# Turning the second block's row maxima on VectorE instead of TensorE

## The chip, the cores and the metric

One core of a Trainium2 chip runs the kernel. Its engines work side by side, each through its own list of instructions in order: TensorE (PE), VectorE (DVE), ScalarE (ACT), GpSimd (POOL) and the queue of SyncE (SP), which issues all transfers. They meet in counting semaphores. The metric is the device time of one execution in microseconds (us), as the median of several runs.

## The reference, cut to what matters

```python
scale = cond @ norm_w.T + 1.0
ms = mean(x * x, axis=-1)
h = x * (scale[:, None, :] * rsqrt(ms + EPS))
u = h @ up_w.T                                  # up_w: 4096 x 512
val, gate = split(u, 2, axis=-1)
h = val * gelu(gate)                            # 4096 rows x 2048
s = 127 / max(max|h| over the row, 1e-5)
hq = clip(round(h * s), -128, 127) / s          # one scale for each row
wq = clip(round(down_w * t), -1, 1) / t         # t: one scale for all of down_w
y = hq @ wq.T + x
```

x has 4 x 1024 rows of 512 numbers. The part around the change is `s`: the row's largest |h|, and from it the row's scale.

## The kernel before, in words

The 4096 rows are worked on in 8 blocks of 512 (`b` = 0 to 7; "second block" is `b` = 1). In a block the hidden dimension 2048 goes in J = 16 tiles of 128. So there are 128 tiles, numbered `n = 16 b + j`. A tile lies with the hidden dimension on the partitions and the block's 512 rows along the free dimension (128x512). Every engine runs one loop over `n`, and its order is written out by hand.

**Tiles 32 to 127** (blocks 2 to 7) make the up product with seven half-size products instead of eight, each in three fp16 passes (lines 582 to 584, 128x256 matmuls of which one starts every 0.11 us). Between the products stand sums that other engines make: ScalarE copies two halves (L803, L806), VectorE adds `seed_gate(n)` (L1135, into `ps_g`) and `second_val(n)` (L1140, into `ps_v`). In round `n` TensorE runs first_pair(n), third(n-1) (waits for seed_gate(n-1)), gates(n-1), second(n), fourth(n-1) (waits for second_val(n-1)). Each round has 42 of these matmuls, 4.58 us. In the first rounds of a block TensorE also makes a quarter of the down product of the block before last (16 matmuls of L709, 3.45 us).

**VectorE** in round `n`: `hidden(n-2)` (L1152: val times gelu), `second_val(n-1)`, `scaled` (L1230: h of the block before times the row scales that stand in the PSUM tile `ps_m`), `peak_of(n-2)` (L1162, L1165: running maximum `h_max`), `residual` (L1251), `seed_gate(n)`, `rounded` (L1237), `sum_low` (L1061), `row_dequant` in round 5 of a block (L1219 or L1223), the norm of the next block (L1101) and the differences of its operands (L1110 to L1124, L1130). `sum_low(k)` belongs to the weights' sums, which are made once, in tiles 20 to 40: POOL sums four parts (L970 to L976), ScalarE makes the high part (L874), VectorE the low part (L1061); SyncE loads the next part (L408) when a buffer is free after `sum_low`. In the third block (tiles 32 to 47) sums 11 to 15 fall in tiles 34, 35, 37, 38 and 40, and all differences of the next block stand in tile 34:

```python
if j == 2:
    difference(b + 1, XT1)
if j == (2 if b < 3 else 4):
    difference(b + 1, XT2)
```

**From the row maxima to the scales.** After the last tile of block `b`, h_max[128, 512] holds for every row 128 partial maxima, one on each partition. There are two ways to the scales, chosen by `by_vector(b)`, which is `V_FIRST <= b < NB - 1`.

- By TensorE (blocks 0, 1 and 7 before): in tile 1 of the next block `turn_max` turns h_max by four transposes into ps_m (L692); in tile 2 VectorE's `row_scales` reduces it (L1206) and makes the scale in three small steps (L1209 to L1213), ahead of its `hidden`; TensorE's `spread_scale` spreads the scales over the partitions by four more transposes (L698).
- By VectorE (blocks 2 to 6 before): in tile 1 `turn_peaks` transposes h_max in 32x32 squares (L1172) and reduces it (L1174); in tile 2, behind `seed_gate`, `spread_peaks` gathers the four quarters with three copies (L1182), reduces them and makes the scale (L1185 to L1193), spreads it with three copies (L1196) and writes ps_m by one transpose (L1200). `row_dequant` then takes four instructions (L1223) instead of one (L1219).

Of the kernel before, what the change touches and what calls it, by code (L numbers as in the profile page):

```python
# [43 lines left out]
def bass_cond_norm_geglu_bitlinear(  # L44
# [83 lines left out]
    RS_DRAM = 5  # L128


    V_FIRST = 2

    def h_home(b, j):
        return J + j if j < 2 and b % 2 == 1 else j
# [1 line left out]
    with ExitStack() as ctx:  # L136
# [176 lines left out]
        def by_vector(b):  # L313
            return V_FIRST <= b < NB - 1

# [710 lines left out]
        def _(dve):  # L1026
# [77 lines left out]
            def difference(c, k):  # L1104
                before = (c - 2) * 4
                if k == XT1:
                    dve.wait_ge(xn_ready, c * KT + 2)
                    if by_vector(c - 2):
                        dve.wait_ge(peak_step, (c - 2 - V_FIRST) * PEAK_STEPS + 1)
                    dve.tensor_tensor(ta[:], xt[:, 0:2, HB:TB], xt[:, 0:2, 0:HB], ALU.subtract).then_inc(t_ready, 1)  # L1110
# [66 lines left out]
            def spread_peaks(b):  # L1177

                base = (b - V_FIRST) * PEAK_STEPS
                dve.wait_ge(peak_step, base + 1)  # L1180
# [249 lines left out]
```

## Time and profile before

| | |
|---|---|
| median of 3 runs | 746.95 us (746.33 to 747.03) |
| the profiled execution | 748.39 us, of which its span is 746.6 us |
| TensorE busy | 732.8 us (98%) |
| VectorE busy | 561.1 us (75%) |
| ScalarE busy | 347.8 us (47%) |
| GpSimd busy | 97.9 us (13%), all before 238 us |

The span runs from the first to the last instruction that the profiler recorded; 1.79 us of the execution lie around it. Times in the rows below are counted from the span's start. The timeline view gives for each entry its start, its length and, in brackets, how long the engine had been idle before it and what ended that.

### The profile page before, as it was taken

What the parts mean: (1) busy time and instruction counts of PE and PEld (TensorE: products, weight loads), DVE (VectorE), ACT (ScalarE), POOL (GpSimd) and SP (SyncE); (2) the same over time, 40 slices, a digit from 0 to 9 for tenths busy, and PEclk for the clock granted to TensorE, in tenths of its full rate; (3) what the DMA queues carried; (4) which work ended last, traced back from release to release, by engine and by line L of the source; (5) the groups of instructions that cost most, each with busy time, mean ns of one, the idle gap of its engine ahead of it and who ended that gap; (6) DMA issues with size and microseconds to landing.
All of it is one profiled execution on the core that took longest, in us unless ns stands there. A gap on an engine that the chain in (4) does not pass through costs nothing.

```text
span 746.6 us, 14329 instructions
## 1 busy us (share of the span) xinstructions
PE 732.8 (98%) x5480; PEld 536.6 (72%) x5480; DVE 561.1 (75%) x1126; ACT 347.8 (47%) x677; POOL 97.9 (13%) x137
## 2 busy tenths in 40 slices
PE   6999999999999999999999999999999999999998
PEld 5544444444677887888778887788878887688864
DVE  5577778998599776888668775887758876586657
ACT  4888866443164532454324643355424442144424
POOL 1211377763314000000000000000000000000000
PEclk9999999999999999999999999999999999999999
DMA  8887574656546444343533444353443333353202
GB/s 321 292 280 235 176 274 135 234 165 233 205 136 183 156 155 149 117 144 99 196 122 126 129 135 157 116 166 104 149 156 103 100 100 125 123 177 103 97 29 84
DMA packets 44788, 117.33 MB, mean 157 GB/s; under 512 B 5424, under 2 KB 5680, under 8 KB 43568
## 3 DMA queue, kind: packets, MB, share of 16 engines
q1 hardware_dynamic: 44720, 116.42, 47.2%
q8 instruction: 43, 0.70, 0.4%
q14 instruction: 25, 0.20, 0.1%
HBM read 99.62 MB, written 16.78 MB: 156 GB/s over the span
## 4 chain that ended last, share of the span: by engine, by line
PE 88%; DVE 5%; ACT 2%; issue 2%; DMA 1%; SPq 0%; DVEq 0%; POOL 0%; ACTq 0%
PE ps_v L582 14%; PE ps_v L584 14%; PE ps_v L583 14%; PE ps_y L709 12%; PE ps_g L582 6%; PE ps_g L584 6%; PE ps_g L583 5%; PE ps_v L600 3%; PE ps_v L602 3%; PE ps_g L602 3%; PE ps_v L601 3%; PE ps_g L601 3%; PE ps_g L600 3%; PE ps_v L778 1%; DMA q<-in_up_t_dram 1%
## 5 line engine op out<-in xcount | busy, mean ns | idle before, releaser
L582 PE MATMUL ps_v<-x_hi,w_hi 128*128 128x256 f16 x968 | 263.9, 273 | 2.9 <-DVE ps_v L1140 1.9
L584 PE MATMUL ps_v<-x_hi,w_lo 128*128 128x256 f16 x968 | 263.8, 273 | 0.0
L583 PE MATMUL ps_v<-x_lo,w_hi 128*128 128x256 f16 x968 | 263.8, 273 | 0.0
L803 ACT COPY ps_g<-ps_v 128x256 f32<-128x256 f32 x96 | 34.3, 357 | 214.9 <-PE ps_v L584 214.9
L814 ACT ACTIVATE g<-ps_g,w_unscale 128x512 f32<-128x512 f32 x128 | 87.3, 682 | 69.5 <-PE ps_g L584 69.4
L1140 DVE TENSOR_TENSOR ps_v<-ps_v,p 128x256 f32<-128x256 f32 x96 | 41.3, 431 | 97.7 <-PE ps_v L584 97.4
L821 ACT ACTIVATE g<-h 128x512 f32<-128x512 f32 x128 | 81.3, 635 | 57.9 <-DVE h L1152 57.4
L582 PEld LDWEIGHTS ps_v<-x_hi,w_hi 128*128 128x128 f16 x968 | 94.7, 98 | 17.9 <-DVE ps_v L1140 2.9
L584 PE MATMUL ps_g<-x_hi,w_lo 128*128 128x256 f16 x392 | 106.8, 273 | 0.0
L582 PE MATMUL ps_g<-x_hi,w_hi 128*128 128x256 f16 x392 | 106.8, 273 | 0.0
L583 PE MATMUL ps_g<-x_lo,w_hi 128*128 128x256 f16 x392 | 106.8, 273 | 0.0
L583 PEld LDWEIGHTS ps_v<-x_lo,w_hi 128*128 128x128 f16 x968 | 94.7, 98 | 13.4
L584 PEld LDWEIGHTS ps_v<-x_hi,w_lo 128*128 128x128 f16 x968 | 94.7, 98 | 11.0
L709 PE MATMUL ps_y<-dw,q 128*128 128x512 bf16 x448 | 101.3, 379 | 0.0
L1152 DVE SCALAR_TENSOR_TENSOR h<-ps_v,w_unscale,g 128x512 f32<-128x512 f32 x128 | 95.3, 744 | 2.4 <-PE ps_v L584 2.2
L1165 DVE TENSOR_TENSOR h_max<-g,h_max 128x512 f32<-128x512 f32 x120 | 84.6, 705 | 12.9 <-ACT g L821 10.2
L1230 DVE TENSOR_TENSOR h<-h,ps_m 128x512 f32<-128x512 f32 x128 | 83.7, 677 | 1.8 <-PE ps_m L698 1.8
L709 PEld LDWEIGHTS ps_y<-dw,q 128*128 128x128 bf16 x448 | 43.8, 98 | 46.8
L1135 DVE TENSOR_TENSOR ps_g<-ps_v,p 128x256 f32<-128x256 f32 x96 | 41.2, 429 | 22.0 <-PE ps_v L584 20.8
L1237 DVE TENSOR_SCALAR q<-h 128x512 bf16<-128x512 f32 x112 | 52.6, 490 | 0.0
L600 PE MATMUL ps_g<-x_hi,w_hi 128*128 128x512 f16 x124 | 47.0, 379 | 0.0
L601 PE MATMUL ps_g<-x_lo,w_hi 128*128 128x512 f16 x124 | 47.0, 379 | 0.0
(139 smaller groups left out, 925.0 us busy)
## 6 DMA issues: line engine op xcount, KB each, us to landing
w_lo<-w_lo_dram SPq DMA_DIRECT2D x96, 448.0 KB, 3.3
q<-in_up_t_dram SPq DMA_DIRECT2D x16, 512.0 KB, 4.9
xt<-in_x_cols_dram SPq DMA_DIRECT2D x8, 1024.0 KB, 4.9
res<-in_x_rows_dram SPq DMA_DIRECT2D x26, 256.0 KB, 3.4
out_dram<-res SPq DMA_DIRECT2D x26, 256.0 KB, 2.7
sums<-in_up_t_dram SPq DMA_DIRECT2D x12, 512.0 KB, 4.7
xs<-in_x_rows_dram SPq DMA_DIRECT2D x22, 256.0 KB, 3.7
w_lo_dram<-w_lo SPq DMA_DIRECT2D x16, 256.0 KB, 4.4
```

What stands on the lines that cost most here:

```text
L582: pe.matmul(to, w_hi[:, wh:wh + P], hi, start=start and kt == 0, stop=False, skip_group_check=True)
L583: pe.matmul(to, w_hi[:, wh:wh + P], lo, start=False, stop=False, skip_group_check=True)
L584: last = pe.matmul(to, w_lo[:, wl:wl + P], hi, start=False, stop=(kt == 1), skip_group_check=True)
L600: pe.matmul(bank, w_hi[:, wh:wh + P], hi, start=start and kt == 0, stop=False)
L601: pe.matmul(bank, w_hi[:, wh:wh + P], lo, start=False, stop=False)
L709: last = pe.matmul(ps_y[:, i % 2, :], q[:, j * TB + i * P:j * TB + (i + 1) * P], dw[:, j * D:(j + 1) * D], start=(j == 0), stop=(j == J - 1))
L814: act.activation(g[:, n % 3, :], ps_g[:, n % NG, :], ACT.Gelu, scale=w_unscale[:, n % J:n % J + 1]).then_inc(g_ready, 1)
L821: act.activation(g[:, n % 3, :], h[:, at:at + TB], ACT.Abs).then_inc(h_abs_ready, 1)
L1152: dve.scalar_tensor_tensor(out=h[:, at:at + TB], in0=ps_v[:, n % NV, :], scalar=w_unscale[:, j:j + 1], in1=g[:, n % 3, :], op0=ALU.mult, o ...
L1165: dve.tensor_tensor(h_max[:], g[:, n % 3, :], h_max[:], ALU.max).then_inc(h_max_ready, 1)
L1230: dve.tensor_tensor(h[:, at:at + TB], h[:, at:at + TB], ps_m[:], ALU.mult).then_inc(scaled_ready, 1)
L1237: dve.tensor_scalar(to[:, j * TB:(j + 1) * TB], h[:, at:at + TB], ROUND, ROUND, ALU.add, ALU.subtract).then_inc(q_ready, 1)
```

## The change

Block 1 too goes by VectorE. On TensorE the calls turn_max(1) and spread_scale(1) go; on VectorE row_scales(1) goes, and turn_peaks(1), spread_peaks(1) and the four-piece form of row_dequant(1) come.

```diff
@@ -128,7 +128,7 @@
     RS_DRAM = 5
 
 
-    V_FIRST = 2
+    V_FIRST = 1
 
     def h_home(b, j):
         return J + j if j < 2 and b % 2 == 1 else j
```

## Rows read from the trace of the kernel before

**Rows 1.** Waits of TensorE over the whole span: us, times, longest.
```profile
PE ps_v L582 <- DVE ps_v L1140: 1.9, 2, 1.5
...
PE ps_v L582 <- DVE ps_g L1135: 0.2, 1, 0.2
```

**Rows 2.** Busy time by stretch: stretch, its length, then each engine.
```profile
230.00:235.00 5.00, 4.90 (x44) 3.93 (x43) 5.00 (x9) 2.89 (x5) 2.00 (x3) 1.00 0.60 166
235.00:240.00 5.00, 3.48 (x33) 2.89 (x31) 5.00 (x9) 1.21 (x2) 2.43 (x3) 1.00 0.28 93
...
292.00:736.00 444.00, 444.00 (x3702) 362.18 (x3701) 332.15 (x703) 181.37 (x382) 0.00 (x0) 1.00 0.38 123
```

**Rows 3.** Timeline of TensorE around the eight transposes of block 1.
```profile
203.82 0.60 PE L692 MATMUL ps_m<-ident,h_max 128*128 128x128 f32 x4
204.25 0.27 PE L582 MATMUL ps_v<-x_hi,w_hi 128*128 128x256 f16 x1
...
212.29 0.60 PE L698 MATMUL ps_m<-ident,row_peak 128*128 128x128 f32 x4
```

**Rows 4.** Timeline of VectorE, tiles 34 and 35.
```profile
204.45 0.69 DVE L1206 TENSOR_REDUCE row_peak<-ps_m 128x4 f32<-128x512 f32 x1 [1.49 <-PE ps_m L692]
...
205.70 0.75 DVE L1152 SCALAR_TENSOR_TENSOR h<-ps_v,w_unscale,g 128x512 f32<-128x512 f32 x1
...
208.38 0.43 DVE L1135 TENSOR_TENSOR ps_g<-ps_v,p 128x256 f32<-128x256 f32 x1
209.49 1.28 DVE L1061 SCALAR_TENSOR_TENSOR xs<-sums,w_scale,w_hi 128x1024 f16<-128x1024 f32 x1 [0.67 <-ACT w_hi L874]
210.69 0.69 DVE L1110 TENSOR_TENSOR ta<-xt 128x512 f32<-128x512 f32 x1
...
218.49 0.42 DVE L1135 TENSOR_TENSOR ps_g<-ps_v,p 128x256 f32<-128x256 f32 x1
```

**Rows 5.** Timeline of TensorE: its waits for VectorE in tiles 35 to 39.
```profile
218.97 0.28 PE L582 MATMUL ps_v<-x_hi,w_hi 128*128 128x256 f16 x1 [0.18 <-DVE ps_g L1135]
...
222.17 0.28 PE L582 MATMUL ps_v<-x_hi,w_hi 128*128 128x256 f16 x1 [0.41 <-DVE ps_v L1140]
...
238.06 0.28 PE L582 MATMUL ps_v<-x_hi,w_hi 128*128 128x256 f16 x1 [1.52 <-DVE ps_v L1140]
```

**Rows 6.** Timeline of VectorE, the turn and the spreading of block 2.
```profile
294.44 0.70 DVE L1172 STREAM_TRANSPOSE ta<-h_max 128x512 f32<-128x512 f32 x1
...
295.78 0.74 DVE L1152 SCALAR_TENSOR_TENSOR h<-ps_v,w_unscale,g 128x512 f32<-128x512 f32 x1
...
299.50 0.43 DVE L1135 TENSOR_TENSOR ps_g<-ps_v,p 128x256 f32<-128x256 f32 x1 [0.33 <-PE ps_v L584]
299.97 0.55 DVE L1182 COPY tb<-tb 32x16 f32<-32x16 f32 x3
...
302.87 0.69 DVE L1110 TENSOR_TENSOR ta<-xt 128x512 f32<-128x512 f32 x1
```

**Rows 7.** Timeline of VectorE, both forms of row_dequant and what follows.
```profile
229.88 0.68 DVE L1219 TENSOR_SCALAR dequant<-row_peak,d_mean 128x4 f32<-128x4 f32 x1
230.48 0.74 DVE L1152 SCALAR_TENSOR_TENSOR h<-ps_v,w_unscale,g 128x512 f32<-128x512 f32 x1
...
317.39 0.97 DVE L1223 TENSOR_SCALAR dequant<-row_peak,d_mean 32x4 f32<-32x4 f32 x4
318.39 0.75 DVE L1152 SCALAR_TENSOR_TENSOR h<-ps_v,w_unscale,g 128x512 f32<-128x512 f32 x1
```

**Rows 8.** Timelines of the SP queue and of POOL: the weights' sums.
```profile
210.80 0.33 SPq L408 DMA_DIRECT2D sums<-in_up_t_dram  x1
...
215.82 0.73 POOL L970 TENSOR_TENSOR sums<-sums 128x256 f32<-128x256 f32 x1 [13.45 <-DMA sums<-in_up_t_dram]
...
228.96 1.58 POOL L976 TENSOR_TENSOR sums<-sums 128x256 f32<-128x256 f32 x1
```

**Rows 9.** One line's instructions: shortest, median and longest in ns.
```profile
L1237 DVE TENSOR_SCALAR q<-h x112: 408/416/986, 123.8 to 707.0; 128x512 bf16<-128x512 f32 x112
```

## The prediction

> **What bounds the kernel now.** I began with the page's shares: TensorE is busy for 98% of the span, so by the page alone anything taken off TensorE looks like a gain. The share is a mean, though, so the next view was that of TensorE's waits over the whole span [rows 1]. After the start-up it waits for VectorE alone, three times, for `second_val` (L1140) and `seed_gate` (L1135). The timeline puts all three into tiles 35 to 39, which is the stretch just behind the change [rows 5]. The view by stretches says why: from 230 to 240 us VectorE is busy for all of both 5 us stretches, and TensorE is not, while from 292 to 736 us TensorE has not one gap [rows 2]. So there are two regimes. Tiles 34 to 39 are VectorE's: it carries the weights' sums (L1061) beside its usual work, and all five differences and low parts of the next block stand in tile 34. Everything behind is TensorE's. A delay that TensorE takes at 238.06 is carried to the end, since no later wait of TensorE exists that could absorb it.
>
> **The change part by part.**
>
> *TensorE loses eight transposes.* The first four take from 203.82 to 204.25, so 0.43 us; the other four have the same recorded length [rows 3]. Together 0.87 us. This is a gain at the end only if TensorE doesn't wait for VectorE afterwards. But at 218.97 it does already, 0.48 us behind the start of the seed at 218.49 [rows 4, 5]. From there on TensorE's time is VectorE's time plus a fixed handover, and being earlier by 0.87 us only makes the wait longer. The one effect of the first four that reaches VectorE is that the products of tile 34 come 0.43 us earlier, and with them seed_gate(34): 208.38 becomes 207.95.
>
> *VectorE, tile 33 and the top of tile 34.* turn_peaks takes 295.78 - 294.44 = 1.34 us [rows 6]. Before, VectorE sat idle for 1.49 us at this place, waiting for TensorE's transposes, and then needed 205.70 - 204.45 = 1.25 us for row_scales [rows 4]. The 1.34 fall in place of 1.49 + 1.25 = 2.74 us. So hidden(32) starts some 1.4 us earlier; but the next two VectorE steps wait for products of TensorE, and seed_gate(34) stands where TensorE puts it. Gain here beyond the 0.43: nothing. If that cover were gone, it would cost 1.34 - 1.25 = 0.09 us.
>
> *VectorE, spread_peaks in tile 34.* Behind the seed the twelve instructions run to the start of the first difference. In block 2 the seed starts at 299.50, the copies at 299.97 and the difference at 302.87: 3.37 us from seed to the next piece of work [rows 6]. In block 1 the piece that follows is sum_low(11), and there VectorE had 209.49 - 208.38 = 1.11 us from seed to sum_low, 0.67 of them waiting for ScalarE's L874 [rows 4]. That wait is used up by the new work, as L874 is long done by 207.95 + 3.37 = 211.32. sum_low(11) moves from 209.49 to 211.32, by 1.83 us. Everything up to the seed of tile 35 at 218.49 is a closed queue behind it, with ScalarE's casts and copies tied to the differences; I find no idle time that could take it up. So seed_gate(35) comes at 220.32, and TensorE's third product of tile 35 at 220.80 instead of 218.97. From this moment both engines are late by the same 1.83 us, so the small gaps that both have in tiles 36 and 37 stay as they are. Put as a difference: 3.37 - 1.11 - 0.43 = 1.83. That is the lower end too, since the steps hang on each other and block 2 ran them with nothing in their way; for the upper end I allow 0.3 us more.
>
> *row_dequant(1) in tile 37.* One instruction becomes four. Clean, the four take 318.39 - 317.39 = 1.00 us; the one that they replace took 230.48 - 229.88 = 0.60 us [rows 7]. That is +0.40 at the least. But the 0.60 was no clean time: the instruction handles four numbers per partition, was recorded with 0.68 us, and ended at 230.56, with a GpSimd instruction that ended at 228.96 + 1.58 = 230.54 [rows 7, 8]. I read this as VectorE held until GpSimd was through. Then the first of the four pieces is held as well (0.68 + 0.03 to the next start), and three clean ones of 0.25 follow: 1.46 - 0.60 = +0.86. I take 0.86, since sums, transfers and VectorE have all moved together by 1.83 and the same instruction of GpSimd should stand there. By the Trainium skill (SBUF — State Buffer, "Who interferes with whom") the two engines share one pair of ports that is locked for a whole instruction, and a tensor_scalar on SBUF can take it; this agrees with the held 0.68, and it speaks against the change, which gives VectorE more of such instructions. By that rule the term is 0.86, without it 0.40.
>
> *Does spread_peaks itself meet GpSimd?* GpSimd's next set of sums starts when its load lands: the load was issued at 210.80, at the end of sum_low(11), and GpSimd began at 215.82 [rows 8]. The load can't be issued before sum_low(11), which now ends behind spread_peaks. So that set starts at about 217.7, in the same place relative to VectorE, and the copies run beside an idle GpSimd. I cost it at nothing. What the queue of SP holds behind that load (a store of y, a load of w_lo for tile 38) is late by the same 1.83 us and is wanted, three tiles on, by a TensorE that is late by as much.
>
> *What is late next.* TensorE's last wait, at 238.06 behind second_val(38), comes at 238.06 + 1.83 + 0.86 = 240.75. From there TensorE is the bound to the end.
>
> *Sum.* +1.83 + 0.86 = +2.69 us against the profiled execution: its span of 746.6 becomes 749.3, its own time of 748.39 about 751.1. The median of the runs shown is 1.44 us below that execution's time; the difference carries over, 746.95 + 2.69 = 749.6 us, or 0.36% slower. About 0.2% (1.5 us) is what a measurement of this kernel can tell from no change.
>
> **The rivals.**
>
> *The sums' contention shrinks (ends not slower).* Dequant now adds 0.86 us behind the issue of the last sums' load, so GpSimd's last set of four instructions meets other VectorE work than before. A rounding (L1237) takes 0.416 us as a rule and 0.986 at the worst [rows 9], so a meeting can cost 0.57; four of them 2.3. If all four that were met now were avoided, the time is 749.6 - 2.3 = 747.3, which is no change. The point at which it decides is 1.2 us less contention. For it: GpSimd is busy for 2.43 us between 235 and 240 while VectorE is full [rows 2], so there is something to avoid. Against it: VectorE is full before and after too, so a GpSimd set that slides by 0.86 us only meets the neighbours of what it meets now. Chance 0.10.
>
> *The contention grows.* The same mechanism in the other direction, 749.6 + 2.3 = 751.9 at the most, and more likely half of it, 750.8. By the same page of the Trainium skill (SBUF — State Buffer, "Who interferes with whom") this would be the rule for the six new copies too, if a set of sums fell on them. No row shows a copy of L1182 beside a busy GpSimd. Chance 0.11 for more than 751.0.
>
> *The new work is hidden.* If VectorE had the slack that its 75% suggest, only TensorE's part remained: 746.95 - 0.87 = 746.1, 0.12% less, no change. Against it stand the two full stretches and the three waits [rows 2, 5]. Chance 0.04.
>
> *Faster.* Needs 0.87 us and 0.6 us more from the waits of tiles 35 to 39, that is, less VectorE work ahead of 218.49 where I count more: 745.4. One way is that the transfers for the sums, now issued later, no longer share the queues and sums and contention both end sooner. Chance 0.03.
>
> **How the numbers follow.** The forecast case (1.83 to 2.1 for spread_peaks, 0.40 to 0.86 for dequant, and half a microsecond of contention and of the median's scatter either way) gives 748.4 to 750.9 and has 0.72. The range 748.1 to 751.0 leaves out the hidden and faster cases, most of the shrunken contention and the far end of the grown one. Slower by over 0.2% (above 748.44) holds the forecast and the grown contention: 0.83; within 0.2%: the hidden case and most of the shrunken one, 0.13; faster 0.04.
>
> **What the profile of the changed kernel would show.** L692 and L698 with 8 instead of 12 matmuls; L1172 and L1182 with 6 and 18 entries, the new L1172 beginning where norm ends (about 203 us) with no idle ahead of hidden(32) but one ahead of the L1140 that follows. seed_gate(34) near 207.95, the first difference near 212.5 (210.69 before). TensorE's waits on L1140 and L1135 grow from 2.1 to about 5.5 us in total, with a new one for L1140 in tile 35, ahead of the one at 220.8; the last near 240.7. Four L1223 near 231.7, the first of them long. From 242 us on every row 2.7 us later. It would be wrong if VectorE showed idle time between sum_low(11) and seed_gate(35), if the three L1182 of block 1 took well above 0.55 us, or if L1237 and L1061 between 233 and 241 us kept or lost another sum than before.

## The result and the profile after

The changed kernel takes 749.87 us (median of 15 runs, 748.99 to 751.33) against 747.01 us for the kernel before (15 runs beside it, 745.55 to 749.03). The ratio is 1.0036, with a 95% interval of 1.0028 to 1.0045. It is slower by 0.36%, which is 2.7 us, as forecast. A few executions among the later runs took 963 us or more, where the rest took about 747; they are left out of the medians and ratios below, and with them one trace, so that 13 are read.

The profiled execution has a span of 747.4 us, only 0.8 us longer than that of before. Here the start has to be taken off first. In round 33 the norm of block 3 (four L1101) starts at 199.31 us in this execution and started at 200.25 in that of before; over the 13 profiles it starts anywhere from 199.23 to 200.78, in kernels that are the same up to there. So I count from that norm, here and in all experiments. From it to the end of the span the kernel before took 746.6 - 200.25 = 546.35 us and the changed one takes 747.4 - 199.31 = 548.09 us: +1.74 us. Spans are given to 0.1 us, so these lengths are good to 0.1 us. Counted to the start of TensorE's last matmuls (L778) they are 541.75 and 543.51 us: +1.76 us.

Part of the scatter of the start-up goes with TensorE's clock. The first 20 us by stretch (stretch, its length, PE, PEld, DVE, ACT, POOL, the granted clock, the DMA share, GB/s), in the kernel before and in the changed one:

```profile
0.00:20.00 20.00, 12.82 (x106) 11.40 (x107) 10.51 (x36) 10.21 (x18) 4.41 (x12) 0.91 0.85 314
```

```profile
0.00:20.00 20.00, 12.80 (x115) 11.31 (x116) 11.31 (x36) 11.03 (x19) 5.45 (x13) 1.00 0.85 316
```

In the first of them the granted clock was 0.50, the lower level of 1.2 GHz, from 13 to 15 us, shortly after TensorE had sat idle for 1.94 us up to 11.69. In the second it stayed at the upper level of 2.4 GHz. From 20 us on it is 1.00 in both, so what is counted from the norm compares like with like. The four traces in which the clock fell in the first 20 us have the norm at 200.09 to 200.78, the nine others at 199.23 to 200.50, so the clock isn't all of the scatter.

The timeline of VectorE in the changed kernel, rounds 33 to 35 (the rows that answer to [rows 4] and [rows 6]):

```profile
201.94 0.70 DVE L1172 STREAM_TRANSPOSE ta<-h_max 128x512 f32<-128x512 f32 x1
...
203.28 0.74 DVE L1152 SCALAR_TENSOR_TENSOR h<-ps_v,w_unscale,g 128x512 f32<-128x512 f32 x1
205.04 0.43 DVE L1140 TENSOR_TENSOR ps_v<-ps_v,p 128x256 f32<-128x256 f32 x1 [1.02 <-PE ps_v L584]
...
207.00 0.43 DVE L1135 TENSOR_TENSOR ps_g<-ps_v,p 128x256 f32<-128x256 f32 x1 [0.32 <-PE ps_v L584]
207.47 0.55 DVE L1182 COPY tb<-tb 32x16 f32<-32x16 f32 x3
...
210.36 1.28 DVE L1061 SCALAR_TENSOR_TENSOR xs<-sums,w_scale,w_hi 128x1024 f16<-128x1024 f32 x1
211.56 0.68 DVE L1110 TENSOR_TENSOR ta<-xt 128x512 f32<-128x512 f32 x1
...
219.00 0.42 DVE L1135 TENSOR_TENSOR ps_g<-ps_v,p 128x256 f32<-128x256 f32 x1
...
230.05 1.44 DVE L1223 TENSOR_SCALAR dequant<-row_peak,d_mean 32x4 f32<-32x4 f32 x4
231.52 0.75 DVE L1152 SCALAR_TENSOR_TENSOR h<-ps_v,w_unscale,g 128x512 f32<-128x512 f32 x1
```

Take off the norm's start, and compare with [rows 4] and [rows 7]. seed_gate(34) comes at 7.69 us instead of 8.13: 0.44 earlier. sum_low(11) comes at 11.05 instead of 9.24: 1.81 later. seed_gate(35) comes at 19.69 instead of 18.24: only 1.45 later, as L1165 ahead of it took 0.68 us instead of 1.03. row_dequant with what it takes up to the next instruction has grown from 0.60 to 231.52 - 230.05 = 1.47 us.

The waits of TensorE over the whole span, and its timeline where they fall (the rows that answer to [rows 1] and [rows 5]):

```profile
PE ps_v L582 <- DVE ps_v L1140: 2.6, 3, 1.3
...
PE ps_v L582 <- ACT p L806: 1.2, 1, 1.2
PE ps_v L582 <- DVE ps_g L1135: 0.6, 1, 0.6
```

```profile
215.52 0.28 PE L582 MATMUL ps_v<-x_hi,w_hi 128*128 128x256 f16 x1 [1.17 <-ACT p L806]
...
216.69 0.28 PE L582 MATMUL ps_v<-x_hi,w_hi 128*128 128x256 f16 x1 [0.34 <-DVE ps_v L1140]
...
219.48 0.28 PE L582 MATMUL ps_v<-x_hi,w_hi 128*128 128x256 f16 x1 [0.65 <-DVE ps_g L1135]
...
232.67 0.28 PE L582 MATMUL ps_v<-x_hi,w_hi 128*128 128x256 f16 x1 [0.99 <-DVE ps_v L1140]
...
238.88 0.28 PE L582 MATMUL ps_v<-x_hi,w_hi 128*128 128x256 f16 x1 [1.29 <-DVE ps_v L1140]
```

The three waits of before have become five, and their sum has grown from 2.1 to 4.4 us. The first is for ScalarE, whose copy (L806) stands behind the casts of the differences, and these wait for VectorE. The last is the same one as before, 39.57 us behind the norm's start instead of 37.81. That is 1.76 us later, and the rest of the kernel carries it (1.74 at the end). TensorE has no gap from 292 to 736 us in either profile.

One step of the forecast did not come true: GpSimd's next set of sums didn't stay in its place beside VectorE's work. Its load and its first instruction in the changed kernel (before: [rows 8]):

```profile
211.67 0.33 SPq L408 DMA_DIRECT2D sums<-in_up_t_dram  x1
...
215.29 0.93 POOL L970 TENSOR_TENSOR sums<-sums 128x256 f32<-128x256 f32 x1 [13.24 <-DMA sums<-in_up_t_dram]
```

Behind the norm, the load is issued at 12.36 us instead of 10.55, so 1.81 later. But GpSimd begins 3.62 us behind the issue instead of 5.02, at 15.98 instead of 15.57, so only 0.41 later. VectorE's work has moved by 1.81 and meets other parts of the set. This isn't the chance of one execution: in the six traces with spread_peaks(1) in round 34 GpSimd begins 3.4 to 3.9 us behind that issue, in the seven others 4.4 to 5.4. Why the load lands sooner there, no run shows.

### The profile page after: what moved, and what is told of

Same layout as the page of the kernel before. It is cut to its first block, busy times and chain, and to the rows that moved or that the text cites. A ratio compares the mean times of both kernels' runs of the same rounds, so it can differ in the third digit from the quotient of the medians.

```text
span 747.4 us, 14329 instructions
## 1 busy us (share of the span) xinstructions
PE 731.4 (98%) x5472; PEld 534.6 (72%) x5472; DVE 564.9 (76%) x1138; ACT 347.6 (47%) x677; POOL 97.9 (13%) x137
## 4 chain that ended last, share of the span: by engine, by line
PE 68%; DVE 2%; issue 1%; DVEq 0%
PE ps_v L582 13%; PE ps_v L584 13%; PE ps_v L583 13%; PE ps_y L709 11%; PE ps_g L582 5%; PE ps_g L584 5%; PE ps_g L583 5%; PE ps_v L778 1%; DVE xs L1061 1%; DVE h L1152 0%; PE ps_g L778 0%; DVE q L1237 0%; DVE ps_v L1140 0%; DVE x_lo L1130 0%; DVE dequant L1223 0%
## 5 line engine op out<-in xcount | busy, mean ns | idle before, releaser
L582 PE MATMUL ps_v<-x_hi,w_hi 128*128 128x256 f16 x968 | 263.9, 273 | 5.1 <-DVE ps_v L1140 2.6
L584 PE MATMUL ps_v<-x_hi,w_lo 128*128 128x256 f16 x968 | 263.8, 273 | 0.0
L1140 DVE TENSOR_TENSOR ps_v<-ps_v,p 128x256 f32<-128x256 f32 x96 | 41.4, 431 | 98.1 <-PE ps_v L584 97.8
L582 PEld LDWEIGHTS ps_v<-x_hi,w_hi 128*128 128x128 f16 x968 | 94.7, 98 | 20.9 <-DVE ps_v L1140 3.8
L582 PE MATMUL ps_g<-x_hi,w_hi 128*128 128x256 f16 x392 | 106.8, 273 | 0.0
L584 PE MATMUL ps_g<-x_hi,w_lo 128*128 128x256 f16 x392 | 106.8, 273 | 0.0
L584 PEld LDWEIGHTS ps_v<-x_hi,w_lo 128*128 128x128 f16 x968 | 94.7, 98 | 11.0
L1165 DVE TENSOR_TENSOR h_max<-g,h_max 128x512 f32<-128x512 f32 x120 | 84.4, 704 | 12.9 <-ACT g L821 10.2
L1237 DVE TENSOR_SCALAR q<-h 128x512 bf16<-128x512 f32 x112 | 52.2, 487 | 0.0
```

The costliest lines, as they stand in the source:

```text
L582: pe.matmul(to, w_hi[:, wh:wh + P], hi, start=start and kt == 0, stop=False, skip_group_check=True)
L584: last = pe.matmul(to, w_lo[:, wl:wl + P], hi, start=False, stop=(kt == 1), skip_group_check=True)
L1165: dve.tensor_tensor(h_max[:], g[:, n % 3, :], h_max[:], ALU.max).then_inc(h_max_ready, 1)
L1237: dve.tensor_scalar(to[:, j * TB:(j + 1) * TB], h[:, at:at + TB], ROUND, ROUND, ALU.add, ALU.subtract).then_inc(q_ready, 1)
```

## The experiments

All of them count from the norm's start. "To the end" is the length from there to the end of the span.

**Whose time is it? GpSimd nearly idle, before and after.** In both kernels GpSimd's sums for k = 13 to 15 are made for one column in 256 only; the rest of them is left out.

```diff
+                if k >= 13:
+                    a21, a22, a11, a12 = [a[:, 0:1] for a in (a21, a22, a11, a12)]
```

> The kernel before, with GpSimd's four sums for k = 13, 14 and 15 made for one column in 256 only (the rest of these sums is left out), so that GpSimd is nearly idle in tiles 34 to 39. Theory: VectorE's stretched instructions there (about 3.6 us in all by the profile of before) become clean, so TensorE's waits in tiles 35 to 39 (3.1 us) nearly vanish: -2.5 to -3.0 us against the kernel before. Rival (the stretched instructions are VectorE's own, not GpSimd's doing): 0.

> The changed kernel with the same part of GpSimd's sums left out. Theory: the difference to the kernel before with the same part left out is the part that has nothing to do with GpSimd, where VectorE is still the bound: 1.83 for spread_peaks and 0.40 for a clean row_dequant, 2.2 us, less what VectorE's regained slack swallows, so between 0.5 and 2.2 us. Rival (the cost of the change is made by meetings with GpSimd): the difference is 0 or -0.87.

Measured: 745.38 us for the one, ratio 0.9978 (0.9968 to 0.9988), and 747.86 us for the other, 1.0006 (0.9996 to 1.0015). The difference is 2.5 us in the medians and 2.1 us by the ratios. To the end: 543.51 and 545.80 us, a difference of 2.29. That is at the upper end of the 0.5 to 2.2 us expected, or just above, and the rival that meetings with GpSimd make the cost is out. The first kernel is 2.8 us shorter to the end than the kernel before in its first profile, 2.2 us shorter than in a second one (below), and 1.6 us faster by the ratio: the direction is the expected one, but the 2.5 to 3.0 us are reached only against the first profile. VectorE's timelines, first the kernel before with small sums, then the changed one:

```profile
217.98 0.42 DVE L1137 TENSOR_TENSOR ps_g<-ps_v,p 128x256 f32<-128x256 f32 x1
...
228.41 0.22 DVE L1221 TENSOR_SCALAR dequant<-row_peak,d_mean 128x4 f32<-128x4 f32 x1
228.54 0.74 DVE L1154 SCALAR_TENSOR_TENSOR h<-ps_v,w_unscale,g 128x512 f32<-128x512 f32 x1
```

```profile
219.10 0.42 DVE L1137 TENSOR_TENSOR ps_g<-ps_v,p 128x256 f32<-128x256 f32 x1
...
229.54 0.97 DVE L1225 TENSOR_SCALAR dequant<-row_peak,d_mean 32x4 f32<-32x4 f32 x4
230.54 0.75 DVE L1154 SCALAR_TENSOR_TENSOR h<-ps_v,w_unscale,g 128x512 f32<-128x512 f32 x1
```

With the norm at 200.09 and 199.40, seed_gate(35) stands at 17.89 and 19.70 us, 1.81 apart, and the `hidden` behind dequant at 28.45 and 31.14, 2.69 apart. These are the two terms of the forecast with nothing else in them: 1.83, and 0.86 for dequant. Of the 2.69 the end shows 2.29, as VectorE in the kernel before with small sums had become early enough for TensorE to be the bound by then. And dequant shows something that the forecast had wrong. With no GpSimd instruction beside it, the single instruction takes 0.13 us to the next start, not 0.60, and the four take 1.00: +0.87, the same as with GpSimd beside it (0.60 to 1.47). So 0.87 is the price either way. The trace of the kernel before had this clean form too, in the last block, long after GpSimd's last instruction:

```profile
723.09 0.22 DVE L1219 TENSOR_SCALAR dequant<-row_peak,d_mean 128x4 f32<-128x4 f32 x1
723.23 0.74 DVE L1251 SCALAR_TENSOR_TENSOR res<-ps_y,dequant,res 128x512 f32<-128x512 f32 x1
```

**Does the sign turn when VectorE is light?** The same sums left out, sum_low for k = 11 to 15 made for 8 columns in 512 only (the rest left out), and the differences of block 3 spread over rounds 34, 36, 39 and 42:

```diff
-                    if j == (2 if b < 3 else 4):
+                    if j == (2 if b < 2 else 4):
                         difference(b + 1, XT2)
```

(and the same edit at the other differences and at ScalarE's casts).

> The kernel before with VectorE made light in tiles 34 to 40: GpSimd's sums for k = 13 to 15 for one column only, VectorE's sum_low for k = 11 to 15 for 8 columns in 512 only (the rest is left out), and the differences of block 3 spread over tiles 34 to 42 as in the later blocks. Theory: no wait of TensorE for VectorE is left in tiles 35 to 39: -3.1 us.

> The changed kernel with the same parts left out and spread. Theory: with VectorE no longer the bound the sign turns, since only TensorE's eight transposes are left of the change: -0.87 us against the kernel before with the same edits. Rival (the VectorE path is slower in itself, wherever it stands): +1 to +2.7 us as before.

Measured: 744.69 us, ratio 0.9968 (0.9955 to 0.9982), and 743.62 us, 0.9954 (0.9939 to 0.997). To the end: 543.27 and 542.42 us. The changed kernel is now the faster one, by 0.85 us where the trace is counted (0.88 to TensorE's last matmuls) and by 1.1 us in the medians. The light kernel before is 3.1 us shorter to the end than the first profile of before, as expected (2.5 against the second one, below). That is more than the 2.1 us that the view of waits shows: a matmul of L582 to L584 is recorded with 0.27 us while the next one starts 0.11 us behind it, so by these rows a wait is shown some 0.16 us too short, and a shorter one not at all. Busy time from 205 to 245 us (stretch, length, then PE, PEld, DVE, ACT, POOL): the kernel before, the changed one, and the same two made light:

```profile
205.00:245.00 40.00, 37.78 (x325) 31.24 (x324) 36.79 (x62) 22.40 (x41) 11.22 (x12) 1.00 0.52 152
```

```profile
205.00:245.00 40.00, 35.49 (x301) 28.61 (x299) 37.02 (x71) 21.33 (x39) 11.72 (x12) 1.00 0.49 149
```

```profile
205.00:245.00 40.00, 40.00 (x354) 34.39 (x352) 31.25 (x67) 23.66 (x43) 2.67 (x12) 1.00 0.53 161
```

```profile
205.00:245.00 40.00, 40.00 (x353) 34.33 (x351) 33.86 (x79) 23.57 (x43) 2.95 (x12) 1.00 0.54 162
```

In the light pair TensorE is busy for all of the 40 us in both, and what is left of the change is its eight transposes. The rival that the VectorE way is slower wherever it stands falls with this.

**One part undone: row_dequant(1) later.**

```diff
-                if 1 <= b < NB and j == 5:
+                if 1 <= b < NB and j == (9 if b == 2 else 5):
                     row_dequant(b - 1)
```

> The changed kernel with row_dequant(1) moved from tile 37 to tile 41, where VectorE is no longer the bound. Theory: the last wait of TensorE (tile 39) comes 1.4 us earlier relative to the start of tile 34 than in the changed kernel (the whole four-piece form, held piece included, leaves the path), so about +1.3 us against the kernel before, 1.0017. Rival (TensorE's fewer transposes and the dequant don't matter, the time comes from elsewhere): no change against the changed kernel.

Measured: 747.16 us, 0.9999 (0.9989 to 1.0009) of the kernel before. To the end: 545.77 us, 2.32 less than the changed kernel, where 1.4 was expected. At the `hidden` behind the place of dequant VectorE stands at 30.51 instead of 32.21 us, 1.70 earlier: 1.47 for dequant, the rest for L1165, L1237 and L1061, which took 3.54 us together instead of 3.41 but closed an idle gap of 0.35 us. More comes in round 38. There the changed kernel, and then this one, have

```profile
234.65 1.51 DVE L1237 TENSOR_SCALAR q<-h 128x512 bf16<-128x512 f32 x2
```

```profile
232.86 0.74 DVE L1237 TENSOR_SCALAR q<-h 128x512 bf16<-128x512 f32 x2
```

with GpSimd's last set starting at 234.29 and 233.30 us. In the changed kernel the two roundings began 0.36 us behind GpSimd, here 0.44 us ahead of it. That is the contention that the forecast had as its uncertain term, and here it gave 0.77 us. Together `second_val(38)` comes 2.48 us earlier. TensorE uses 2.3 of them: its waits of 0.99 and 1.29 us in rounds 38 and 39 are gone, and the last one shown is that in round 35.

**The changed kernel again,** as control of these runs.

> The changed kernel itself, as the control of the three that follow. Theory (VectorE is the bound in tiles 34 to 39, so its extra work counts one for one): +2.7 us against the kernel before, ratio 1.0036, of which 1.83 us arise at seed_gate(35) and 0.86 in row_dequant. In the first profile the part of the weights' sums' contention came out 0.9 us smaller than in the profile of before; if that holds for every run, this kernel is nearer +1.8 us (1.0024). Rival (the extra time is a start-up difference between builds): nothing of the ratio shows in tiles 34 to 39.

Measured: 749.80 us as the median of five executions, 2.4 us above the kernel before beside it; ratio 1.004 (1.0025 to 1.0055). The effect repeats. Five executions hardly tell 1.0036 from 1.0024, and this build has no trace to read, so the control says nothing on where its time arises.

**TensorE's transposes put back.** Four transposes of h_max into ps_m in round 33, as turn_max(1) had them, whose result nobody uses.

```diff
+            def turn_idle(b):
+                pe.wait_ge(h_max_ready, (b + 1) * J)
+                pe.wait_ge(xn_ready, min(b + 3, RS_DRAM) * KT)
+                pe.wait_ge(scaled_ready, b * J)
+                for i in range(TT):
+                    last = pe.transpose(ps_m[:, i * P:(i + 1) * P], h_max[:, i * P:(i + 1) * P], ident[:])
+                last.then_inc(idle_turned, 1)
...
+                if b == 2 and j == 1:
+                    turn_idle(b - 1)
...
+                    if b == 2:
+                        dve.wait_ge(idle_turned, 1)
```

> The changed kernel, with the four transposes of turn_max(1) put back on TensorE in tile 33 as extra work that nobody uses (VectorE waits for them before it overwrites h_max). Theory: they push the products of tile 34 and so seed_gate(34) by 0.43 us, and all behind it, since this is the one place where TensorE's time still reaches VectorE: +0.43 us against the changed kernel. Rival (VectorE's queue alone sets the time): 0.0 us.

Measured: 750.05 us, 1.0036 (1.0022 to 1.005). To the end: 548.10 us against 548.09 of the changed kernel. Up to round 35 the theory holds to 0.01 us: seed_gate(34) at 8.13 instead of 7.69, seed_gate(35) at 20.13 instead of 19.69. By `hidden` in round 38 it is gone (32.08 against 32.21): in round 37 the rounding took 0.42 instead of 0.99 us and sum_low(13) 1.32 instead of 1.74. A delay in front of the meetings with GpSimd moved VectorE out of one of them. So the end shows the rival's 0.0 us, but not for the rival's reason: TensorE's transposes did reach VectorE. One execution shows this; another may fall otherwise, and the ratios can't tell 0.4 us.

**spread_peaks(1) in round 33,** directly behind turn_peaks(1).

```diff
-                if 1 <= b < NB and j == 2 and by_vector(b - 1):
+                if 3 <= b < NB and j == 2 and by_vector(b - 1):
                     spread_peaks(b - 1)
...
                     turn_peaks(b - 1)
+                    if b == 2:
+                        spread_peaks(b - 1)
```

> The changed kernel with spread_peaks(1) run directly behind turn_peaks(1) in tile 33 instead of behind seed_gate(34). The same instructions on the same engine, but the 1.02 + 0.32 us in which VectorE idled in front of second_val(33) and seed_gate(34) are now filled. Theory: hidden(32) starts 2.9 us later, second_val(33) waits up to 1.8 us longer, seed_gate(34) some 0.3 to 1.6 us later, but sum_low(11) comes about 1.3 us earlier than in the changed kernel: -1.3 us, so +1.4 us against the kernel before. Rival (what counts is only that TensorE is held up early): slower than the changed kernel by the new wait for second_val(33), +0.5 to +1.8 us.

Measured: 748.9 us, 1.0025 (1.0016 to 1.0034). To the end: 547.43 us, 0.66 less than the changed kernel; in the medians about 1.0 less. Its VectorE and TensorE:

```profile
206.45 0.75 DVE L1152 SCALAR_TENSOR_TENSOR h<-ps_v,w_unscale,g 128x512 f32<-128x512 f32 x1
...
209.51 1.28 DVE L1061 SCALAR_TENSOR_TENSOR xs<-sums,w_scale,w_hi 128x1024 f16<-128x1024 f32 x1 [0.19 <-ACT w_hi L874]
```

```profile
207.60 0.28 PE L582 MATMUL ps_v<-x_hi,w_hi 128*128 128x256 f16 x1 [0.47 <-DVE ps_v L1140]
```

TensorE now waits earlier, for 0.47 us more, and this costs nothing: the kernel still gains, because sum_low(11) stands at 10.04 instead of 11.05 us, 1.0 us earlier. In this full stretch it is the place of VectorE's queue that counts. The gain falls short of the expected 1.3 by two waits for ScalarE (0.36 us ahead of L1162, 0.19 us ahead of sum_low(11)) and then by a meeting with GpSimd (L1165 took 1.03 us instead of 0.68, and seed_gate(35) stands at 19.03, 0.66 earlier only).

**The kernel before, profiled again.**

> The kernel before once more, for a second profile. The median of many runs puts the change at +2.8 us, while the two profiles, counted from the start of the norm of block 3 (L1101 in tile 33) to the end, differ by 1.74 us only. Theory A (GpSimd's meetings with VectorE fall differently from one execution to the next): up to the rounding in tile 35 every step repeats within 0.02 us, and the length from the norm to the end differs from the first profile's 546.35 us by some tenths, through stretched L1165, L1237 and L1061 alone; 545.3 us would close the gap. Theory B (the length repeats, and the gap is one of start-up): 546.35 again.

To the end: 545.74 us, 0.61 less than in the first profile, while its steps up to second_val(34) stand within 0.01 us of those of the first. The difference comes from peak_of in round 35 (0.80 instead of 1.03 us) and from L1237 and L1061 in round 37. So theory A holds in kind: against this profile the change costs 548.09 - 545.74 = 2.35 us. It doesn't close the gap to the runs; 0.4 us between 2.35 and 2.7 stay unexplained, no more than the half width of the interval (0.6 us). Part of it may be the clock of the start-up: the nine executions of the changed kernel with a granted clock of 1.0 average 749.50 us, and those of the kernel before with 0.999 or more, in three later sets, 746.86 to 747.06, which puts the change at 2.4 to 2.6 us.

**Spread the differences out: the kernel before, then the changed one with dequant in round 41 too, then that with spread_peaks in round 33 as well.** Nothing is left out in these.

> The kernel before, with the differences of block 3 spread over tiles 34, 36, 39 and 42 on VectorE and their casts on ScalarE to match, as in the later blocks. Nothing is left out. Theory: of the 3.3 us moved out of tile 34, XT3, XN4 and one low part (1.9 us) leave the stretch ahead of TensorE's last wait, so its 3.1 us of waits shrink by 1.9: -1.9 us against the kernel before. Rival (the order within the full stretch does not matter): 0.

> The changed kernel with the differences of block 3 spread out in the same way and row_dequant(1) in tile 41. Theory: +2.7 from the change, -1.4 from dequant, -1.9 from the spreading: -0.6 us against the kernel before at least; if the waits of TensorE vanish altogether, all of 3.1 + 0.87, so -3.9 us. In both cases the change would be worth having only if this beats the kernel before with the same spreading, by up to 0.87 us.

> The same with spread_peaks(1) run in tile 33 as well, where VectorE idled. Theory: in the changed kernel that move gained 0.7 us by profile (1.3 us by medians); here VectorE has more slack behind it, so it gains less or loses the 0.5 us that TensorE then waits for second_val(33): between -0.7 and +0.5 us against the kernel of the run before.

Measured: 746.66 us, 0.999 (0.998 to 0.9999); 745.67 us, 0.9983 (0.9973 to 0.9992); 746.25 us, 0.9988 (0.9978 to 0.9999). To the end: 544.38, 544.27 and 545.03 us. The first misses its number, the second lies between its bounds, the third just outside of them. The spreading alone gains 0.6 us in the medians, where 1.9 was expected, and 1.4 to 2.0 to the end. With it and the later dequant the change is no longer a loss; it is ahead by 1.0 us in the medians and by 0.1 to 0.2 in the traces, with intervals that overlap, so a gain isn't shown. The third is behind the second by 0.6 and 0.8 us: with slack behind it, the early wait for second_val(33) is a loss after all. What still holds TensorE in the second one is mostly a meeting in round 35, behind which it waits for 1.03 us:

```profile
217.62 1.69 DVE L1237 TENSOR_SCALAR q<-h 128x512 bf16<-128x512 f32 x2
219.24 1.74 DVE L1061 SCALAR_TENSOR_TENSOR xs<-sums,w_scale,w_hi 128x1024 f16<-128x1024 f32 x1
```

These took 0.76 and 1.28 us in the changed kernel. The second kernel of the three is the fastest complete one measured, ahead of the kernel before by 0.17%.

## Why the prediction was right, step by step

- **VectorE is the bound in rounds 34 to 39, TensorE behind them.** Shown: with VectorE made light, TensorE has no gap, and the change gains 0.85 us instead of losing.
- **TensorE's 0.87 us are worth nothing here but for the first 0.43.** Shown in both directions: seed_gate(34) moved by 0.44, and moved back by 0.44 when the transposes were put back; the whole 0.87 came out only in the light pair (0.85 to 0.88).
- **turn_peaks is covered.** It took 203.28 - 201.94 = 1.34 us, and VectorE idled for 1.02 us behind it.
- **spread_peaks, +1.83 at sum_low(11).** Measured +1.81, in the plain pair and in the pair with small sums.
- **GpSimd's set keeps its place: wrong.** The forecast let it start 1.83 us later, with everything else; it started 0.41 us later, as its load landed sooner. On this step stood the assumption that contention stays as it was, and that the same GpSimd instruction would hold dequant. Contention changed; dequant was held all the same.
- **row_dequant, +0.86.** Measured +0.87, twice. The size was right and part of the reasoning was not, so the agreement is partly luck. The forecast took 0.40 for the clean case, because the clean form of the single instruction was not in its rows. It takes 0.13 us to the next start, so the four cost 0.87 also where GpSimd is silent. That the 0.68 us were a wait for GpSimd is shown by the same pair: 0.22 us without it. The rule of the port pair (the Trainium skill, SBUF — State Buffer, "Who interferes with whom") decided nothing about this term.
- **Contention, taken as unchanged.** It wasn't: L1165 and L1237 gave back 0.92 us between the first two profiles (0.35 and 0.34 in round 35, 0.23 in round 38), and meetings took or gave 0.4 to 1.0 us in the variants. The 0.23 us are one of the signs that the forecast had named for being wrong. The part in round 35 has a pattern: with all differences in tile 34 and full sums, the two roundings there took 1.10 us in the three traces in which the load is slow and 0.75 to 0.76 in the three in which it lands sooner. This is the mechanism of the rival "contention shrinks", at less than its 1.2 us. The sum of the two terms is 2.69 and the ratio says 2.7, but its interval of 2.1 to 3.4 also holds the 2.34 to 2.35 us of the second pair of profiles. So the runs confirm the two terms, and not that contention cancels out.
- **The waits of TensorE,** forecast at about 5.5 us by the view of waits, are 4.4; most of what is missing is the 0.9 us of contention that this execution gave back. The one expected for L1140 in round 35 came in two pieces, the larger of them for ScalarE's copy L806 that stood behind the delayed casts.
- **Slips in the sums.** The terms of the forecast case add up to 748.7 to 750.4 us with half a microsecond to either side, or 748.2 to 750.9 with half a microsecond each for contention and scatter; the 748.4 to 750.9 of the text is neither. The time of the faster case is 746.95 - 0.87 - 0.60 = 745.5, not 745.4. The differences and low parts in tile 34 are six instructions, four and two, not five. None of these moves the forecast.

## What to carry to other kernels

A kernel whose matrix engine is busy for 98% can still have a stretch in which another engine is the bound, and work moved onto that engine in that stretch counts one for one, while what it frees on the matrix engine is worth nothing. Before work is moved, find the last wait behind the place where it goes: who is waited for there decides, and only what stands ahead of that wait costs. Here the same move gains 0.85 us where VectorE has slack (shown with part of its work left out) and loses 2.7 where it hasn't (1.7 to 2.4 between single executions). Moving one tiny four-piece step behind the last wait took the loss away: 1.5 us by itself, the rest through meetings with GpSimd that it changed.

When everything behind a step is late by the same amount, ask whether each transfer is too. Here the one that starts GpSimd's next set landed sooner, and so the set met other work.

Compare two profiles from a common landmark behind the start-up, not by their spans; here the start-up alone scattered by 1.5 us, in part, it seems, because TensorE's clock fell in it in some executions and not in others.

## What the runs showed of the hardware

- Four instructions on 32 partitions each take 1.00 us on VectorE where one on 128 partitions takes 0.13 us to the next start, with four numbers per partition in both. The four start 0.25 us apart.
- An instruction of four numbers per partition (L1219) took 0.68 to 0.69 us beside a busy GpSimd and 0.22 us beside an idle one, and a 128x512 rounding (L1237) up to 0.99 instead of 0.42.
- Such meetings can swallow a delay: in one execution 0.44 us put in ahead of them in round 33 had vanished by round 38.
- The same load (L408, 512 KB) let GpSimd begin 3.4 to 3.9 us behind its issue in the six traces with spread_peaks(1) in round 34 ahead of it, and 4.4 to 5.4 us in the seven others; why is open.
- In a start-up in which TensorE sat idle for 1.94 us, its granted clock was 0.50 for two microseconds soon after; in the changed kernel's profiled start-up it stayed at 1.00.
